# Rounded gate and sigmoid kept as 16-bit halves of a shifted fp32 word, and three-bank evictions, in the quantised feed-forward network at the end of an audio tower

## The chip, the cores and the metric

The kernel runs on one core of one Trainium2 chip. The metric is the device time of one execution in microseconds, from the first to the last instruction with what lies around them. Engines: PE is TensorE (PEld its weight loads), DVE is VectorE, ACT is ScalarE, POOL is GpSimd, SP is the queue that issues the DMAs of this part.

## The reference, cut to what matters

The tower turns audio into 8 x 376 tokens of 256 features, then runs attention, a mixture of experts, a recurrence, and last a feed-forward network in which every step is rounded to 16 bits with one scale for the whole tensor. Only this last network matters here:

```python
def act_qdq(x):
    scale = jnp.maximum(jnp.max(jnp.abs(x)) / 32767, 1e-12)
    return jnp.clip(jnp.round(x / scale), -32768, 32767) * scale
def fixed_qdq_u16(x):
    return jnp.clip(jnp.round(x * 65536), 0.0, 65535.0) / 65536
x = act_qdq(x)
up = act_qdq(x @ dequant(w_up).T)          # 256 -> 768
gate = act_qdq(x @ dequant(w_gate).T)      # 256 -> 768
sig = fixed_qdq_u16(sigmoid(gate))
gate = act_qdq(gate * sig)
o = act_qdq(gate * up)
out = h + o @ dequant(w_down).T            # 768 -> 256
```

Each `act_qdq` needs the largest absolute value of the whole tensor before the first element of it can be rounded. So the network has five points at which everything waits for a peak: x, gate, up, gate*sig and the product with up.

## The kernel before, in words

The last network is the function `quantised_ffn`. A tensor lies as 128 partitions by 6 chunks (QCHUNKS) by 3008 tokens, 8 samples (BATCH) of 376 tokens (TOK). `gate` stays in SBUF whole as fp32. `up` has room for three samples (UPS); the first five samples of it go out to DRAM and come back. Every product on TensorE is three matmuls (high by high, high by low, low by high part). Each engine has its own program; semaphores tie them. A unit is half a sample: 3 chunks, 1128 elements in each partition; there are 16 units.

**Peaks.** `measure` (DVE, L2018 to L2034) reduces the collected peaks, has TensorE turn and spread the top (`share`, L1889 and L1891), and writes a scale and its inverse (L2029, L2030).

**Gate stage.** DVE rounds x by adding MAGIC (1.5 * 2^23; `rounded`, L2038), ACT takes MAGIC off into the high part (`raise_q`, L1939), DVE makes the low part (`lower`, L2043). PE makes the gate in 48 chunks of six matmuls (`chunk`, L1901) into six PSUM banks. ACT evicts each chunk alone (`keep`, L1952), and after the fourth chunk of each sample it makes the high part of the next sample. DVE takes the peak of each sample (`gate_peak`, L2047).

**Sigmoid stage.** PE makes the 48 chunks of `up`. Per unit: ACT adds MAGIC to the scaled gate (`scale_gate`, L1956); DVE takes MAGIC off and scales it back (`ready_gate`, L2061); ACT makes the sigmoid (L1963); POOL multiplies it by 65536 and adds MAGIC (`scale_sig`, L2152); DVE clips it and takes MAGIC off (`ready_sig`, L2067); POOL multiplies gate and sigmoid (`weigh`, L2157); ACT evicts three chunks of `up` (L1952); DVE takes the peak of up (`up_peak`, L2047) and of the gate times sigmoid (`act_peak`, L2072). The sigmoids lie in a ring of four.

**Multiply stage.** Per sample: ACT rounds up (`round_up`, L1970) and gate (`scale_act`, L1974) to packed int16 in `ints`, two buffers each; DVE multiplies them into fp32 (`multiply`, L2079) and takes the peak (`out_peak`, L2083).

**Product stage.** Per sample: DVE rounds (`round_product`, L2089), ACT makes the high part (`high_product`, L1981), DVE the low part (`low_product`, L2094), PE multiplies with the down weights in three token tiles of 18 matmuls each (`product`, L1915), DVE adds the result to the rows loaded late (`result`, L2104), SP stores.

SP stores and reloads `up` in sample order and waits for the same counts of evictions and roundings as ACT makes them.

Of the kernel before, what the change touches and what calls it, by code (L numbers as in the profile page):

```python
# [1784 lines left out]
SIG_STEPS = 65536.0  # L1785
TINY = 1e-12
# [22 lines left out]
def quantised_ffn(nc, psum, norm, up, peaks_x, a, consts, ident, up_gate, down, late_rows, out):  # L1809
# [5 lines left out]
    with ctx:  # L1815
# [9 lines left out]
            .rearrange("p (w u c n) -> p w u c n", w=2, u=2, n=TOK)  # L1825
        gate = sb("q_gate", [P, QCHUNKS, TOKENS])
        peaks = sb("q_peaks", [P, 4, UNITS])
# [4 lines left out]
        steps = sb("q_steps", [P, 12])  # L1832
        (S_X, I_X, S_UP, I_UP, S_GATE, I_GATE, S_ACT, I_ACT, S_BOTH, S_OUT, I_OUT, PEAK) = (
            steps[:, i:i + 1] for i in range(12))
# [7 lines left out]
         gate_scaled, gate_ready, sig_made, sig_scaled, sig_ready, prod_made, act_scaled, up_rounded, out_made,  # L1842
# [3 lines left out]
            "gate_scaled gate_ready sig_made sig_scaled sig_ready prod_made act_scaled up_rounded out_made "  # L1846
# [7 lines left out]
        with nc.Block() as block:  # L1854
            @block.sync
            def _(sp):
                def store(n):
                    u = n % 2
                    sp.wait_ge(result_made, TILES * (n + 1))
                    many, few = token_rows(out, n)  # L1860
                    sp.dma_start(many, late[:, u, 0:2, :]).then_inc(stored[u], 16)
                    sp.dma_start(few, late[0:TILE_ROWS[2], u, 2, :]).then_inc(stored[u], 16)

                for n in range(BATCH - UPS):
                    sp.wait_ge(kept, CHUNKS_ALL + QCHUNKS * (n + 1))
# [70 lines left out]
            def _(act):  # L1936
# [5 lines left out]
                def keep(t):  # L1942
                    n, j = t // QCHUNKS % BATCH, t % QCHUNKS
                    act.wait_ge(made, t + 1)
                    if t < CHUNKS_ALL:
                        dst = gate[:, j, tokens_of(n)]
                    else:
                        dst = up[:, slot(n), j, :]
                        if j == 0 and n >= UPS:
# [8 lines left out]
                def sigmoid(m):  # L1958
                    c, t = half(m)
                    act.wait_ge(gate_ready, m + 1)  # L1960
                    if m >= RING:
                        act.wait_ge(prod_made, m - RING + 1)
                    act.activation(sig[:, m % RING, :, :], gate[:, c, t], ACT.Sigmoid).then_inc(sig_made, 1)  # L1963

                def round_up(k):
                    if k >= UPS:
                        act.wait_ge(up_in[late_slot(k)], 16 * (k // UPS))
                    if k >= 2:
                        act.wait_ge(out_made, k - 1)
                    act.activation(ints[:, 0, k % 2, :, :], up[:, late_slot(k), :, :], ACT.Copy,  # L1970
                                   scale=I_UP).then_inc(up_rounded, 1)
# [5 lines left out]
                def high_product(n):  # L1977
                    act.wait_ge(p_made, n + 1)
                    if n >= 2:
                        act.wait_ge(down_made, TILES * (n - 1))  # L1980
                    act.activation(prod_high[:, n % 2, :, :], shared[:, n % 2, :, :], ACT.Identity,  # L1981
# [23 lines left out]
                for n in range(BATCH):  # L2005
                    high_product(n)

            @block.vector
            def _(dve):
# [40 lines left out]
                def gate_peak(n):  # L2050
                    dve.wait_ge(kept, QCHUNKS * (n + 1))
                    peak_of(GATE_, n, gate[:, :, tokens_of(n)])

                def up_peak(m):
                    dve.wait_ge(kept, CHUNKS_ALL + UNIT * (m + 1))
                    peak_of(UP_, m, up[:, slot(m // 2), half(m)[0], :])

                def ready_gate(m):
                    c, t = half(m)
                    dve.wait_ge(gate_scaled, m + 1)  # L2060
                    dve.tensor_scalar(gate[:, c, t], gate[:, c, t], MAGIC, S_GATE, ALU.subtract,  # L2061
                                      ALU.mult).then_inc(gate_ready, 1)

                def ready_sig(m):
                    s = sig[:, m % RING, :, :]
                    dve.wait_ge(sig_scaled, m + 1)
                    dve.tensor_scalar(s, s, MAGIC + SIG_STEPS - 1, MAGIC, ALU.min, ALU.subtract).then_inc(sig_ready, 1)  # L2067

# [6 lines left out]
                def multiply(k):  # L2075
                    g = gate[:, :, tokens_of(order[k])]
# [9 lines left out]
                def round_product(n):  # L2086
                    if n >= 2:
                        dve.wait_ge(p_low, n - 1)
                    dve.tensor_scalar(shared[:, n % 2, :, :], gate[:, :, tokens_of(n)], I_OUT, MAGIC,  # L2089
                                      ALU.mult, ALU.add).then_inc(p_made, 1)  # L2090

                def low_product(n):
                    dve.wait_ge(p_high, n + 1)
                    dve.scalar_tensor_tensor(prod_low[:, n % 2, :, :], shared[:, n % 2, :, :], MAGIC,  # L2094
                                             prod_high[:, n % 2, :, :].bitcast(F32), ALU.subtract,
# [34 lines left out]
                act_peak(UNITS - 1)  # L2130
                measure(STEP_ACT, peaks[:, ACT_, :], S_ACT, I_ACT, (ranged, UNITS))
                link(dve.tensor_scalar(S_BOTH, S_ACT, S_UP, 1.0 / SIG_STEPS, ALU.mult, ALU.mult))
# [6 lines left out]
                low_product(0)  # L2139
                for n in range(BATCH):  # L2140
                    if n + 2 < BATCH:
                        round_product(n + 2)
                    if n + 1 < BATCH:
                        low_product(n + 1)
                    result(n)

            @block.gpsimd
            def _(pool):
                def scale_sig(m):
                    s = sig[:, m % RING, :, :]  # L2150
                    pool.wait_ge(sig_made, m + 1)
                    pool.tensor_scalar(s, s, SIG_STEPS, MAGIC, ALU.mult, ALU.add).then_inc(sig_scaled, 1)  # L2152

                def weigh(m):
                    c, t = half(m)
                    pool.wait_ge(sig_ready, m + 1)
                    pool.tensor_tensor(gate[:, c, t], gate[:, c, t], sig[:, m % RING, :, :], ALU.mult).then_inc(prod_made, 1)  # L2157

                for m in range(UNITS + 1):
                    if m < UNITS:  # L2160
                        scale_sig(m)
                    if m:
                        weigh(m - 1)
# [142 lines left out]
```

## Time and profile before

| what | value |
|---|---|
| median of 3 runs | 1931.11 us (1928.57 to 1936.67) |
| profiled execution, time | 1944.91 us |
| profiled execution, span | 1943.1 us |
| busy share of the span | PE 82%, PEld 76%, DVE 63%, ACT 52%, POOL 58% |
| mean granted TensorE clock | 0.902 of full speed |

The span runs from the first to the last instruction; the execution's own time is 1.8 us more. The busy shares are means over stages with different limits, so what a change in the last network can bring is read from its own stretch, about 1684 to 1943 us. A granted clock of 1.00 is 2.4 GHz, 0.50 is 1.2 GHz.

### The profile page before, as it was taken

What the parts mean: (1) busy time and instruction counts of PE and PEld (TensorE: products, weight loads), DVE (VectorE), ACT (ScalarE), POOL (GpSimd) and SP (SyncE); (2) the same over time, 40 slices, a digit from 0 to 9 for tenths busy, and PEclk for the clock granted to TensorE, in tenths of its full rate; (3) what the DMA queues carried; (4) which work ended last, traced back from release to release, by engine and by line L of the source; (5) the groups of instructions that cost most, each with busy time, mean ns of one, the idle gap of its engine ahead of it and who ended that gap; (6) DMA issues with size and microseconds to landing.
All of it is one profiled execution on the core that took longest, in us unless ns stands there. A gap on an engine that the chain in (4) does not pass through costs nothing. (4 is left out here: it accounts for less than half of the span.)

```text
span 1943.1 us, 32428 instructions
## 1 busy us (share of the span) xinstructions
PE 1594.4 (82%) x11205; PEld 1479.0 (76%) x11205; DVE 1228.0 (63%) x2392; ACT 1018.9 (52%) x2231; POOL 1120.1 (58%) x859
## 2 busy tenths in 40 slices
PE   7749999999999999997519999999999826698219
PEld 4338898989898989896419999999999825687119
DVE  6756575757575757474624666666655468558886
ACT  3536564647474746473515555554555424459452
POOL 0487676767585858580546767667677646107500
PEclk9859999999999999997559999999999957899659
DMA  5153000000000000000336555555555421003123
GB/s 189 64 188 102 1 8 0 8 0 8 0 8 0 8 8 0 8 2 28 106 113 192 147 143 135 148 136 138 143 151 149 109 77 32 25 1 120 48 87 112
DMA packets 74600, 142.85 MB, mean 74 GB/s; under 512 B 7400, under 2 KB 50728, under 8 KB 73992
## 3 DMA queue, kind: packets, MB, share of 16 engines
q1 hardware_dynamic: 63992, 127.80, 21.0%
q0 software_dynamic: 10512, 13.83, 4.3%
q8 instruction: 53, 0.87, 0.2%
q14 instruction: 43, 0.35, 0.1%
HBM read 108.15 MB, written 46.83 MB: 80 GB/s over the span
## 5 line engine op out<-in xcount | busy, mean ns | idle before, releaser
L1463 POOL TENSOR_TENSOR expert_w_low<-expert_raw,expert_w_high 128x768 fp32r<-128x768 f32 x152 | 289.8, 1959 | 158.4 <-ACT expert_w_high L1322 157.3
L646 ACT ACTIVATE probs<-psum,neg_max 120x376 f32<-120x376 f32 (+2 forms) x384 | 176.3, 479 | 138.6 <-DVE neg_max L763 138.6
L716 POOL TENSOR_TENSOR qk_low<-rotated,qk_high 128x376 fp32r<-128x376 f32 x128 | 138.5, 1082 | 178.7 <-ACT qk_high L639 174.5
L533 PE MATMUL psum<-diag,probs 128*128 128x128 f32 (+2 forms) x1536 | 204.0, 284 | 26.9 <-DVE pt_low L779 22.6
L533 PEld LDWEIGHTS psum<-diag,probs 128*128 128x128 f32 (+2 forms) x1536 | 185.9, 194 | 36.0 <-issue 25.1
L779 DVE TENSOR_TENSOR pt_low<-psum,pt_high 128x752 fp32r<-128x752 f32 x128 | 120.4, 941 | 144.1 <-ACT pt_high L655 143.1
L1439 DVE TENSOR_TENSOR expert_act_low<-expert_act,expert_act_high 128x384 fp32r<-128x384 f32 x152 | 148.3, 976 | 79.6 <-ACT expert_act_high L1360 79.6
L1360 ACT ACTIVATE expert_act_high<-expert_act 128x384 fp32r<-128x384 f32 x152 | 79.8, 525 | 171.4 <-DVE expert_act L1434 171.4
L1281 PE MATMUL psum<-slots_high,expert_w_high 128*128 128x384 f32 x608 | 158.3, 341 | 9.0 <-DVE expert_act L1434 7.8
L1281 PE MATMUL psum<-slots_low,expert_w_high 128*128 128x384 f32 x608 | 155.6, 337 | 0.0
L1281 PE MATMUL psum<-slots_high,expert_w_low 128*128 128x384 f32 x608 | 155.5, 336 | 0.0
L655 ACT ACTIVATE pt_high<-psum 128x752 fp32r<-128x752 f32 x128 | 102.6, 802 | 98.3 <-PE psum L533 96.7
L727 POOL TENSOR_TENSOR rotated<-raw,rope_cos 128x376 f32<-128x376 f32 x128 | 127.5, 996 | 39.3 <-ACT raw L633 25.4
L731 POOL TENSOR_TENSOR rotated<-rotated,swapped 128x376 f32<-128x376 f32 x128 | 138.5, 1082 | 10.0
L1322 ACT ACTIVATE expert_w_high<-expert_raw 128x768 fp32r<-128x768 f32 x152 | 126.6, 833 | 30.3 <-DMA expert_raw<-in_experts 30.3
L1292 PE MATMUL psum<-expert_w_high,expert_act_high 128*128 128x256 f32 x456 | 134.3, 294 | 5.2 <-ACT slot_out L1342 3.8
L1434 DVE TENSOR_TENSOR expert_act<-psum,silu 128x384 f32<-128x384 f32 x152 | 84.6, 557 | 78.6 <-ACT silu L1356 78.2
L729 POOL TENSOR_TENSOR swapped<-swapped,rope_sin 128x376 f32<-128x376 f32 x128 | 132.7, 1037 | 0.0
L1292 PE MATMUL psum<-expert_w_high,expert_act_low 128*128 128x256 f32 x456 | 128.5, 282 | 0.0
L1292 PE MATMUL psum<-expert_w_low,expert_act_high 128*128 128x256 f32 x456 | 128.4, 282 | 0.0
L763 DVE TENSOR_REDUCE neg_max<-psum 120x2 f32<-120x752 f32 (+2 forms) x192 | 119.1, 676 | 4.6 <-PE psum L518 4.6
L550 PE MATMUL psum<-pt_high,v_high 128*128 128x376 f32 (+2 forms) x384 | 114.7, 299 | 1.7 <-DVE pt_low L779 1.7
(304 smaller groups left out, 4633.3 us busy)
## 6 DMA issues: line engine op xcount, KB each, us to landing
expert_raw<-in_experts SPq DMA_DIRECT2D x152, 384.0 KB, 3.1
x_slots<-in_c_slots SPq DMA_DIRECT2D x4, 3168.0 KB, 28.2
slot_rows<-x_slots SPq DMA_DIRECT2D x19, 396.0 KB, 4.4
up_spill<-held SPq DMA_DIRECT2D x5, 1128.0 KB, 5.0
held<-up_spill SPq DMA_DIRECT2D x5, 1128.0 KB, 5.6
patch<-in_patches SPq DMA_DIRECT2D x4, 752.0 KB, 6.7
hid_spill<-hid SPq DMA_DIRECT2D x1, 3008.0 KB, 8.5
resid<-hid_spill SPq DMA_DIRECT2D x8, 376.0 KB, 3.5
```

The source lines that it names most:

```text
L533: last = pe.matmul(psum[0:nj, BANK_PT + bank, at:at + ni], probs[0:ni, h % 2, src:src + nj], diag[0:ni, h % 2, it, 0:ni], start=True, stop ...
L646: last = act.activation(probs[0:ni, h % 2, at:at + P * it + ni], score_bank(h % 2, it), ACT.Exp, bias=neg_max[0:ni, h % 2, it:it + 1], acc ...
L716: pool.tensor_tensor(qk[1][:, c % 2, k, :], rotated[:, k, :], qk[0][:, c % 2, k, :].bitcast(F32), ALU.subtract).then_inc(qk_ready, 1)
L727: pool.tensor_tensor(rotated[:, k, :], raw[:, k, :], cos[:], ALU.mult).then_inc(rope_made, 1)
L729: pool.tensor_tensor(swapped[:, k, :], swapped[:, k, :], sin[:], ALU.mult).then_inc(rope_made, 1)
L731: pool.tensor_tensor(rotated[:, k, :], rotated[:, k, :], swapped[:, k, :], ALU.add).then_inc(rot_made, 1)
L779: dve.tensor_tensor(pt[1][:, h % 2, :, :], psum[:, BANK_PT:BANK_PT + 2, 0:TOK], pt[0][:, h % 2, :, :].bitcast(F32), ALU.subtract).then_inc ...
L1281: last = pe.matmul(psum[:, 2 * k + g % 2, 0:TILE_SLOTS], w[hw][:, f, at:at + P], xt[hx][:, i % 2, c, :], start=(n == c == 0), stop=(n == 2 ...
L1292: last = pe.matmul(psum[:, BANK_DOWN + s, 0:DIM], act_hl[ha][:, g % 2, P * s:P * (s + 1)], w[hw][:, f, 4 * P:4 * P + DIM], start=(n == f = ...
L1322: act.activation(w[0][:, g % RING, :], raw[:, g % RAW, :], ACT.Copy).then_inc(w_high, 1)
L1439: dve.tensor_tensor(act_hl[1][:, g % 2, :], act_f[:, g % 2, :], act_hl[0][:, g % 2, :].bitcast(F32), ALU.subtract).then_inc(low_made, 1)
L1463: pool.tensor_tensor(w[1][:, g % RING, :], raw[:, g % RAW, :], w[0][:, g % RING, :].bitcast(F32), ALU.subtract).then_inc(w_low, 1)
```

## The change

All of it lies in `quantised_ffn`.

- The gate is scaled and MAGIC added as before, but MAGIC is not taken off again. The low 16 bits of the word are the rounded integer: `gate_low` reads them as int16 at a step of two halves. The sigmoid (ACT) reads them with the scale S_GATE.
- The sigmoid is rounded by adding SIG_MAGIC = MAGIC / 65536 = 192 and clipped, in one DVE instruction; the low 16 bits of that word are the integer, read as uint16 (`sig_low`).
- The product of the two halves is now DVE's. POOL has no instruction in this function any more.
- ACT evicts three PSUM banks with one instruction, in both stages; PE signals and waits once in three chunks. The high part of the next sample comes before the first eviction of a sample.
- `scale_act` writes int16 into the low halves of `gate` in place; `ints` holds four roundings of up. The first two roundings of up wait for the scale of up alone.
- The product of the first sample is prepared in two pieces (128 tokens, then 248), and PE waits before each token tile for what it needs.
- The peak of gate*sig is now one of integers, so its `measure` has two more small steps (S_PROD).

```diff
+SIG_MAGIC = MAGIC / SIG_STEPS
+        sig_low = shared[:]...bitcast(mybir.dt.uint16).rearrange("p (r c n w) -> p r c n w", r=RING, c=UNIT, w=2)[:, :, :, :, 0]
+        gate_low = gate[:]...bitcast(mybir.dt.int16).rearrange("p (c n w) -> p c n w", c=QCHUNKS, w=2)[:, :, :, 0]
+        pieces = [(0, 0, P), (0, P, TOK)] + [(n, 0, TOK) for n in range(1, BATCH)]
...
 # PE, chunk(t)
-                    if t >= BANKS:
-                        pe.wait_ge(kept, t - BANKS + 1)
+                    if j % UNIT == 0 and t >= BANKS:
+                        pe.wait_ge(kept, t // UNIT - 1)
...
-                    last.then_inc(made, 1)
+                    if j % UNIT == UNIT - 1:
+                        last.then_inc(made, 1)
 # PE, product(n)
-                    pe.wait_ge(p_low, n + 1)
...
                     for t in range(TILES):
+                        pe.wait_ge(p_low, n + 2 if n or t else 1)
 # ACT
-                    act.activation(dst, psum[:, j % BANKS, 0:TOK], ACT.Copy, scale=S_X).then_inc(kept, 1)
+                    act.activation(dst, psum[:, c, 0:TOK], ACT.Copy, scale=S_X).then_inc(kept, 1)
...
-                    act.activation(sig[:, m % RING, :, :], gate[:, c, t], ACT.Sigmoid).then_inc(sig_made, 1)
+                    act.activation(sig[:, m % RING, :, :], gate_low[:, c, t], ACT.Sigmoid, scale=S_GATE).then_inc(sig_made, 1)
...
-                    act.activation(ints[:, 1, k % 2, :, :], gate[:, :, tokens_of(order[k])], ACT.Copy,
-                                   scale=I_ACT).then_inc(act_scaled, 1)
+                    act.activation(gate_low[:, :, t], gate[:, :, t], ACT.Copy, scale=I_ACT).then_inc(act_scaled, 1)
...
-                for t in range(CHUNKS_ALL):
-                    keep(t)
-                    if t % QCHUNKS == 3 and t // QCHUNKS + 1 < BATCH:
-                        raise_q(t // QCHUNKS + 1)
+                for m in range(UNITS):
+                    if m % 2 == 0 and m // 2 + 1 < BATCH:
+                        raise_q(m // 2 + 1)
+                    keep(m)
                 act.wait_ge(steps_made, STEP_GATE + 1)
                 scale_gate(0)
-                scale_gate(1)
                 for m in range(UNITS):
-                    if m + 2 < UNITS:
-                        scale_gate(m + 2)
+                    if m + 1 < UNITS:
+                        scale_gate(m + 1)
                     sigmoid(m)
-                    for j in range(UNIT):
-                        keep(CHUNKS_ALL + UNIT * m + j)
+                    keep(UNITS + m)
+                act.wait_ge(steps_made, STEP_UP + 1)
+                round_up(0)
+                round_up(1)
                 act.wait_ge(steps_made, STEP_ACT + 1)
-                round_up(0)
                 for k in range(BATCH):
                     scale_act(k)
-                    if k + 1 < BATCH:
-                        round_up(k + 1)
+                    if k + 2 < BATCH:
+                        round_up(k + 2)
 # DVE
-                def ready_gate(m):
...
-                    dve.tensor_scalar(s, s, MAGIC + SIG_STEPS - 1, MAGIC, ALU.min, ALU.subtract).then_inc(sig_ready, 1)
+                    dve.tensor_scalar(s, s, SIG_MAGIC, SIG_MAGIC + 1 - 1 / SIG_STEPS, ALU.add, ALU.min).then_inc(sig_ready, 1)
+                def weigh(m):
...
+                    dve.tensor_tensor(gate[:, c, t], gate_low[:, c, t], sig_low[:, m % RING, :, :], ALU.mult).then_inc(prod_made, 1)
...
-                    dve.tensor_tensor(g, ints[:, 1, k % 2, :, :], ints[:, 0, k % 2, :, :], ALU.mult).then_inc(out_made, 1)
+                    dve.tensor_tensor(gate[:, :, t], gate_low[:, :, t], ints[:, k % RING, :, :], ALU.mult).then_inc(out_made, 1)
...
-                ready_gate(0)
-                ready_gate(1)
-                for m in range(UNITS + 1):
-                    if m + 2 < UNITS:
-                        ready_gate(m + 2)
+                for m in range(UNITS):
+                    ready_sig(m)
                     if m:
-                        ready_sig(m - 1)
-                        up_peak(m - 1)
-                    if m >= 3:
-                        act_peak(m - 3)
+                        act_peak(m - 1)
+                    weigh(m)
+                    up_peak(m)
                 measure(STEP_UP, peaks[:, UP_, :], S_UP, I_UP, (peaked, BATCH + UNITS))
-                act_peak(UNITS - 2)
                 act_peak(UNITS - 1)
-            @block.gpsimd
-                    pool.tensor_scalar(s, s, SIG_STEPS, MAGIC, ALU.mult, ALU.add).then_inc(sig_scaled, 1)
-                    pool.tensor_tensor(gate[:, c, t], gate[:, c, t], sig[:, m % RING, :, :], ALU.mult).then_inc(prod_made, 1)
```

## Rows read from the trace of the kernel before

**Rows 1.** Sigmoid and product stage: PE, PEld, DVE, ACT, POOL busy; clock; DMA, GB/s.

```profile
1745.30:1827.30 82.00, 51.99 (x276) 48.15 (x274) 75.34 (x64) 60.62 (x81) 64.20 (x32) 0.88 0.20 71
1886.40:1939.40 53.00, 52.94 (x432) 52.72 (x432) 35.42 (x36) 13.10 (x6) 0.00 (x0) 0.97 0.32 95
```

**Rows 2.** Chain that ended last, gate stage: start us, duration us, what.

```profile
1684.12 6.32 PE psum L1901 x24
...
1692.88 4.44 PE psum L1901 x24
...
1697.34 0.57 ACT q_gate L1952
1697.92 0.82 ACT q_tokens_high L1939
...
1698.76 0.95 DVE q_tokens_low L2043
...
1699.76 4.43 PE psum L1901 x24
...
1734.02 6.52 PE psum L1901 x36
```

**Rows 3.** ACT: a one-bank eviction, and a two-bank one just before this network.

```profile
L1952 ACT ACTIVATE q_gate<-psum,q_steps 128x376 f32<-128x376 f32 x48 | 27.5, 574 | 25.5 <-PE psum L1901 25.5
L1644 ACT ACTIVATE held<-psum 128x752 f32<-128x752 f32 x8 | 6.4, 797 | 8.3 <-PE psum L1578 8.3
```

**Rows 4.** Timeline of ACT, start of the sigmoid stage: start, duration, then the instruction.

```profile
1745.37 3.77 ACT L1956 ACTIVATE q_gate<-q_gate,consts,q_steps 128x1128 f32<-128x1128 f32 x3 [4.23 <-DVE q_steps L2030]
1749.17 1.28 ACT L1963 ACT_TABLE_LOAD   x1
1750.46 1.14 ACT L1963 ACTIVATE q_shared<-q_gate 128x1128 f32<-128x1128 f32 x1
```

**Rows 5.** Timeline of DVE in the sigmoid stage: its start, middle and end.

```profile
1755.16 0.73 DVE L2067 TENSOR_SCALAR q_shared<-q_shared 128x1128 f32<-128x1128 f32 x1
1755.81 1.32 DVE L2047 TENSOR_REDUCE q_peaks<-held 128x1 f32<-128x1128 f32 x1
...
1768.63 1.11 DVE L2061 TENSOR_SCALAR q_gate<-q_gate,q_steps 128x1128 f32<-128x1128 f32 x1
1769.67 1.29 DVE L2067 TENSOR_SCALAR q_shared<-q_shared 128x1128 f32<-128x1128 f32 x1
1770.88 1.31 DVE L2047 TENSOR_REDUCE q_peaks<-held 128x1 f32<-128x1128 f32 x1
...
1773.35 1.14 DVE L2061 TENSOR_SCALAR q_gate<-q_gate,q_steps 128x1128 f32<-128x1128 f32 x1
...
1827.29 0.15 DVE L2021 TENSOR_REDUCE q_own<-q_peaks 128x1 f32<-128x16 f32 x1
```

**Rows 6.** Timeline of ACT (one row) and DVE around the start of the multiply stage.

```profile
1829.24 2.56 DVE L2072 TENSOR_REDUCE q_peaks<-q_gate 128x1 f32<-128x1128 f32 x2
...
1833.82 2.17 ACT L1970 ACTIVATE q_shared<-held,q_steps 128x2256 int16<-128x2256 f32 x1 [19.06 <-DVE q_steps L2030]
...
1838.15 2.51 DVE L2079 TENSOR_TENSOR q_gate<-q_shared 128x2256 f32<-128x2256 int16 x1 [4.11 <-ACT q_shared L1974]
...
1843.11 2.50 DVE L2079 TENSOR_TENSOR q_gate<-q_shared 128x2256 f32<-128x2256 int16 x1
```

**Rows 7.** Chain that ended last, from the last scale on.

```profile
1880.25 1.41 DVE q_shared L2089
...
1883.88 2.52 DVE q_tokens_low L2094
...
1886.45 52.95 PE psum L1915 x432
```

**Rows 8.** DVE, 384 elements of two SBUF operands, beside POOL's work and without it.

```profile
L1439 DVE TENSOR_TENSOR expert_act_low<-expert_act,expert_act_high 128x384 fp32r<-128x384 f32 x152 | 148.3, 976 | 79.6 <-ACT expert_act_high L1360 79.6
L1425 DVE TENSOR_TENSOR q_raw<-q_raw,q_scale 128x384 f32<-128x384 f32 x12 | 6.7, 558 | 0.4
```

More of the change, by code:

```diff
@@ L1824, in quantised_ffn @@
         ints = shared[:].rearrange("p u c n -> p (u c n)").bitcast(mybir.dt.int16) \
-            .rearrange("p (w u c n) -> p w u c n", w=2, u=2, n=TOK)
+            .rearrange("p (u c n) -> p u c n", u=RING, n=TOK)
+        sig_low = shared[:].rearrange("p u c n -> p (u c n)").bitcast(mybir.dt.uint16) \
+            .rearrange("p (r c n w) -> p r c n w", r=RING, c=UNIT, w=2)[:, :, :, :, 0]
         gate = sb("q_gate", [P, QCHUNKS, TOKENS])
+        gate_low = gate[:].rearrange("p c n -> p (c n)").bitcast(mybir.dt.int16) \
+            .rearrange("p (c n w) -> p c n w", c=QCHUNKS, w=2)[:, :, :, 0]
         peaks = sb("q_peaks", [P, 4, UNITS])
@@ L1831, in quantised_ffn @@
         late = sb("q_late", [P, 2, TILES, DIM])
-        steps = sb("q_steps", [P, 12])
-        (S_X, I_X, S_UP, I_UP, S_GATE, I_GATE, S_ACT, I_ACT, S_BOTH, S_OUT, I_OUT, PEAK) = (
-            steps[:, i:i + 1] for i in range(12))
+        steps = sb("q_steps", [P, 13])
+        (S_X, I_X, S_UP, I_UP, S_GATE, I_GATE, S_ACT, I_ACT, S_BOTH, S_OUT, I_OUT, PEAK, S_PROD) = (
+            steps[:, i:i + 1] for i in range(13))
+        pieces = [(0, 0, P), (0, P, TOK)] + [(n, 0, TOK) for n in range(1, BATCH)]
         magic, minus_magic = consts[:, PLUS_MAGIC:PLUS_MAGIC + 1], consts[:, MINUS_MAGIC:MINUS_MAGIC + 1]
@@ L1940, in raise_q, with keep @@
                                    bias=minus_magic).then_inc(high_made, 1)
[L1942 to L1946, printed above, removed]
-                    else:
-                        dst = up[:, slot(n), j, :]
-                        if j == 0 and n >= UPS:
+                def keep(m):
+                    n, (c, t) = m // 2 % BATCH, half(m % UNITS)
+                    act.wait_ge(made, m + 1)
+                    if m < UNITS:
+                        dst = gate[:, c, t]
+                    else:
+                        dst = up[:, slot(n), c, :]
+                        if m % 2 == 0 and n >= UPS:
                             act.wait_ge(up_out[slot(n)], 16 * (n // UPS))
                             act.wait_ge(peaked, BATCH + 2 * (n - UPS + 1))
-                    act.activation(dst, psum[:, j % BANKS, 0:TOK], ACT.Copy, scale=S_X).then_inc(kept, 1)
+                    act.activation(dst, psum[:, c, 0:TOK], ACT.Copy, scale=S_X).then_inc(kept, 1)
                 def scale_gate(m):
@@ L1959, in sigmoid @@
                     c, t = half(m)
-                    act.wait_ge(gate_ready, m + 1)
+                    act.wait_ge(gate_scaled, m + 1)
                     if m >= RING:
                         act.wait_ge(prod_made, m - RING + 1)
-                    act.activation(sig[:, m % RING, :, :], gate[:, c, t], ACT.Sigmoid).then_inc(sig_made, 1)
+                    act.activation(sig[:, m % RING, :, :], gate_low[:, c, t], ACT.Sigmoid, scale=S_GATE).then_inc(sig_made, 1)
                 def round_up(k):
@@ L1967, in round_up, with high_product @@
                         act.wait_ge(up_in[late_slot(k)], 16 * (k // UPS))
-                    if k >= 2:
-                        act.wait_ge(out_made, k - 1)
-                    act.activation(ints[:, 0, k % 2, :, :], up[:, late_slot(k), :, :], ACT.Copy,
+                    if k >= RING:
+                        act.wait_ge(out_made, k - RING + 1)
+                    act.activation(ints[:, k % RING, :, :], up[:, late_slot(k), :, :], ACT.Copy,
                                    scale=I_UP).then_inc(up_rounded, 1)
                 def scale_act(k):
-                    act.activation(ints[:, 1, k % 2, :, :], gate[:, :, tokens_of(order[k])], ACT.Copy,
-                                   scale=I_ACT).then_inc(act_scaled, 1)
-                def high_product(n):
-                    act.wait_ge(p_made, n + 1)
+                    t = tokens_of(order[k])
+                    act.activation(gate_low[:, :, t], gate[:, :, t], ACT.Copy, scale=I_ACT).then_inc(act_scaled, 1)
+                def high_product(i):
+                    n, lo, hi = pieces[i]
+                    act.wait_ge(p_made, i + 1)
                     if n >= 2:
                         act.wait_ge(down_made, TILES * (n - 1))
-                    act.activation(prod_high[:, n % 2, :, :], shared[:, n % 2, :, :], ACT.Identity,
+                    act.activation(prod_high[:, n % 2, :, lo:hi], shared[:, n % 2, :, lo:hi], ACT.Identity,
                                    bias=minus_magic).then_inc(p_high, 1)
@@ L2075, in multiply @@
                 def multiply(k):
-                    g = gate[:, :, tokens_of(order[k])]
+                    t = tokens_of(order[k])
                     dve.wait_ge(act_scaled, k + 1)
                     dve.wait_ge(up_rounded, k + 1)
-                    dve.tensor_tensor(g, ints[:, 1, k % 2, :, :], ints[:, 0, k % 2, :, :], ALU.mult).then_inc(out_made, 1)
+                    dve.tensor_tensor(gate[:, :, t], gate_low[:, :, t], ints[:, k % RING, :, :], ALU.mult).then_inc(out_made, 1)
                 def out_peak(k):
@@ L2117, in _ @@
                 measure(STEP_GATE, peaks[:, GATE_, 0:BATCH], S_GATE, I_GATE, (peaked, BATCH))
-                ready_gate(0)
-                ready_gate(1)
-                for m in range(UNITS + 1):
-                    if m + 2 < UNITS:
-                        ready_gate(m + 2)
+                link(dve.tensor_scalar(S_PROD, S_GATE, 1.0 / SIG_STEPS, None, ALU.mult))
+                for m in range(UNITS):
+                    ready_sig(m)
                     if m:
-                        ready_sig(m - 1)
-                        up_peak(m - 1)
-                    if m >= 3:
-                        act_peak(m - 3)
+                        act_peak(m - 1)
+                    weigh(m)
+                    up_peak(m)
                 measure(STEP_UP, peaks[:, UP_, :], S_UP, I_UP, (peaked, BATCH + UNITS))
-                act_peak(UNITS - 2)
                 act_peak(UNITS - 1)
-                measure(STEP_ACT, peaks[:, ACT_, :], S_ACT, I_ACT, (ranged, UNITS))
-                link(dve.tensor_scalar(S_BOTH, S_ACT, S_UP, 1.0 / SIG_STEPS, ALU.mult, ALU.mult))
+                measure(STEP_ACT, peaks[:, ACT_, :], S_ACT, I_ACT, (ranged, UNITS), S_PROD)
+                link(dve.tensor_tensor(S_BOTH, S_ACT, S_UP, ALU.mult))
                 for k in range(BATCH):
@@ L2139, in _ @@
                 low_product(0)
+                round_product(2)
+                low_product(1)
                 for n in range(BATCH):
                     if n + 2 < BATCH:
-                        round_product(n + 2)
+                        round_product(n + 3)
                     if n + 1 < BATCH:
-                        low_product(n + 1)
+                        low_product(n + 2)
                     result(n)
-            @block.gpsimd
[L2148 to L2151, printed above, removed]
-                    pool.tensor_scalar(s, s, SIG_STEPS, MAGIC, ALU.mult, ALU.add).then_inc(sig_scaled, 1)
-                def weigh(m):
-                    c, t = half(m)
-                    pool.wait_ge(sig_ready, m + 1)
-                    pool.tensor_tensor(gate[:, c, t], gate[:, c, t], sig[:, m % RING, :, :], ALU.mult).then_inc(prod_made, 1)
[L2159 to L2163, printed above, removed]
 def audio_tower(nc, a, out):
```

38 lines of the change are left out of this document (19 added, 19 removed).

## The prediction

> **What bounds the kernel now.** I read the stretches first, then the chain of waits that ended last, then the timelines of DVE and ACT where the chain sits on them. Nothing before 1684 us changes, so only the last network counts. The chain shows four stages in it, each bounded by something else.
>
> Gate stage: 48 chunks of six matmuls. The reader is to see that a sample takes 6.88 us (1692.88 to 1699.76), though 36 matmuls without a break take 6.52 us [rows 2]: the last ones of a sample are waited out because ACT made the next high part only after the fourth eviction, and DVE the low part behind it.
>
> Sigmoid stage: DVE is busy 75.3 of 82.0 us and PE only 52.0 [rows 1]. From 1768.63 to 1773.35 stands one period of 4.72 us with four DVE instructions and no gap [rows 5]. POOL is busy 64.2 us beside it [rows 1], and the same `ready_sig` that occupies DVE for 1.21 us in the middle (1769.67 to 1770.88) took 0.65 us at the start (1755.16 to 1755.81), when POOL had nothing to do [rows 5].
>
> Multiply stage: DVE again, multiply and peak, one sample in 4.96 us (1838.15 to 1843.11) [rows 6].
>
> Product stage: PE without a break, 52.95 us for 432 matmuls, behind a lead of 6.20 us (1880.25 to 1886.45) in which it has nothing [rows 7].
>
> **The change part by part.**
>
> *Gate stage.* One matmul takes (6.52 - 4.43) / 12 = 0.174 us, so a sample 6.27 us if nothing stops PE [rows 2]. Is it stopped? After the change DVE does per sample rounding, a peak and a low part, some 4.1 us; ACT a high part (0.82 [rows 2]) and two evictions. The next low part is ready 1.2 (eviction) + 2.5 (peak) + 0.95 = 4.7 us into a sample, before the 6.27 are over. Two halves of three banks are enough, since a half is evicted in about 1.2 us and needed again after 3.1. So PE runs through: the first sample at the low clock takes 6.32 + 12 x 0.174 = 8.4 us, seven more 43.9: 52.3 against 56.4 now (1684.12 to 1734.02 + 6.52). Gain 4.1. The last eviction is longer. One bank takes 0.57 us, two 0.80 [rows 3]; a third adds at least the 0.22 between these and at most a whole 0.57, so 1.0 to 1.4, and I take 1.2, because ACT takes 1.26 for 1128 elements of SBUF (3.77 / 3 [rows 4]). That is 0.6 later. **Net -3.5 us.**
>
> *Sigmoid stage.* Now it runs from 1745.37 to 1827.29 [rows 4, 5], 81.9 us. Its start: two `scale_gate` (2.5), the table load (1.28), a sigmoid (1.14) [rows 4]: DVE begins 5.0 us in. Per unit DVE then has
> - `ready_sig` without POOL: 0.65, against 1.21 now [rows 5];
> - `weigh`, new on DVE. No row has an operand of 16-bit halves at a step of two. The nearest is the multiplication of packed int16 into fp32, 2.51 us for 2256 elements [rows 6], so half of it, 1.25. Its bounds: not below 0.65 (the fastest DVE pass over 1128 elements in the trace [rows 5]), and above twice the row, 2.5, if halves at a step were read at half speed. I take 1.25, as the element count is the same and the bytes spanned are those of fp32;
> - two peaks, 1.23 each [rows 5]. `ready_gate` (1.04) is gone.
>
> Sum 4.36 us against 4.72. The first unit has no `act_peak` and waits some 0.3 for the second sigmoid: 3.4; fifteen more 65.4. With the start 73.8. **-8.1 us.** What covers the rest: ACT has 1.26 + 1.04 + 1.2 = 3.5 us in a unit, PE 18 x 0.174 = 3.1, so neither is next; the next is ACT, 0.9 behind. The sigmoid waits for the `weigh` four units back, which DVE has then done. The stores of `up` go by counts that are reached as before, and a slot is wanted again only three samples (26 us) later. The extra link for S_PROD lies in DVE's wait for the first sigmoid.
>
> *Start of the multiply stage.* From the last peak of up (1827.29 [rows 5]) to the first multiplication (1838.15 [rows 6]) are 10.86 us: 1.95 for the scale, then two peaks of 1.28 each on DVE, a second scale, and then two ACT roundings (1833.82 to 1838.15, 4.33). After: ACT rounds `up` twice as soon as the scale of up stands, and the scale of the act needs one peak, 2.0 and two more small steps, in all about 3.7 us, under the 4.2 of the two roundings. So 1.95 + 3 roundings (6.4) = 8.35. **-2.5 us.** The two steps of S_PROD thus cost nothing; without that cover they would be 0.4. The reloads of `up` start earlier by as much, and none of the five was waited for before.
>
> *Multiply stage.* DVE again has both instructions per sample, 4.96 us. `multiply` reads one operand at a step; bounds as above, taken at its row. ACT, writing halves at a step, has two roundings of 2.07, 4.14 us, and 0.8 of slack. **0.**
>
> *Product stage.* For 128 tokens (768 elements a partition) the lead is rounding 0.6 (L2089's 1.41 cut to a third), high part 0.85, low part 0.95 (the 752-element ones took 0.82 and 0.95 [rows 2]), with waits 2.6 us against 6.20. DVE's next steps, two roundings and the low part of 248 tokens, end about 5.5 us after the scale. PE's first 18 matmuls, at the low clock, took 3.7 us of the 52.95, so they end at 6.3: no new wait. If the second piece were late, each us would count. After that the order is that of before. **-3.6 us.**
>
> *Evictions and signals.* 96 evictions become 32 and PE's waits a third. All of it is on ACT and PE, which bound no stage but the first, where it is counted.
>
> Sum: 3.5 + 8.1 + 2.5 + 3.6 = 17.7 us. The profiled execution has a span of 1943.1 and took 1944.91 us; it would take 1927.2. The median of the runs is 13.8 us under it; I take the same 17.7 from the median, 1931.11: **1913.4 us**.
>
> **The rules.** `ready_sig` at 0.65 rests on POOL being the cause of the 1.21. A second place shows the same for two operands: 384 elements took 976 ns beside POOL and 558 without it [rows 8]. The Trainium skill (SBUF — State Buffer, Who interferes with whom) says that GpSimd and a two-port VectorE instruction take one port pair in turns, each for a whole instruction; by that the 1.21 goes with POOL. On 16-bit operands at a step the Trainium skill (Advanced Engine Details and Errata, SBUF Cachelines) says full speed as long as successive accesses share a 16-byte line; a step of 4 bytes does, so by it the sum stays 17.7. No row here tests it.
>
> **The rivals.**
> - *Halves at a step are read slowly on DVE.* At twice the time `weigh` adds 1.25 x 16 = 20 us and `multiply` 2.5 x 8 = 20, both on the engine that bounds its stage: 1913.4 + 40 = 1953.4, slower than before. It decides from a factor of 1.44 on. For it: no row has such an operand. Against: packed 16-bit, fp32 and peaks all go at one element in about 1.1 ns. Chance 0.05.
> - *ACT writes or reads halves slowly.* `scale_act` at 4.1 makes ACT 6.2 per sample against 4.96: 6 x 1.25 + 2.1 = 9.6; the sigmoids at 2.1 make ACT 4.5 a unit against 4.36, 2 us and 1 at the start. 1926. Chance 0.05.
> - *POOL was not the cause.* `ready_sig` stays at 1.21: 16 x 0.56 = 9 us: 1922.4. Against it are the two pairs of rows named. Chance 0.05.
> - *PE takes over in the sigmoid stage.* It now waits for three banks at once. At the lower of its two clocks 18 matmuls take at least three quarters of the 6.32 of the first 24 [rows 2], 4.7, and at most twice 3.13, 6.3, both over 4.36; I take 5.5. The granted clock of the stage is 0.88, with PE busy 63% [rows 1]; with a shorter period PE is busier, 71%. If it stayed low for all: (5.5 - 4.36) x 15 = 17 us, so 1931, no change. Chance 0.04.
> - That the change does not do what it says would be seen as POOL instructions in the stage; the diff leaves none.
>
> **How the numbers follow.** The forecast has 0.81. About 0.5% (9.7 us) is what a measurement of this kernel tells from no change; faster means under 1921.5. All of the forecast and a part of the POOL rival lie there: 0.83. Same: the rest of that rival, the ACT and PE ones, 0.12. Slower: the first rival, 0.05. The range: down by 2 us for eviction and periods and 5 for the spread of the runs, whose lowest lies 2.5 under the median, 1906; up to the ACT rival, 1926. Left out are the DVE and PE rivals and a tail below.
>
> **What would show it.** No POOL in the stretch; DVE's `ready_sig` at about 0.73 and `weigh` at about 1.3; a period of 4.36 in the sigmoid stage; PE in the gate stage without gaps; three-bank evictions at 1.2; the first multiplication 8.4 us after the last peak of up; PE starting 2.6 us after the last scale. A `weigh` or `multiply` at double length, or gaps in DVE's row of the sigmoid stage, would make the prediction wrong.

## The result, and the profile after

The changed kernel takes 1913.97 us (median of 4 runs, 1912.91 to 1914.82), the kernel before 1931.56 us in the same comparison: a ratio of 0.9911, 95% interval 0.9899 to 0.9923, so 17.6 us or 0.9% less. The forecast was 1913.4. One execution of kernel 11 below took 2693.7 us at a granted clock of 0.551 and is left out of its median.

The two profiled spans lie 30.1 us apart (1943.1 and 1913.0), more than the change is worth. Counted from the first gate matmul to the end of the last product, the network took 255.3 us before (1684.12 to 1939.40 [rows 2, 7]) and takes 238.3 now (1671.08 to 1909.34). The other 13 us lie ahead of it, in code that is the same in both: the profiled execution before was itself 13 us above the median of the kernel before, the one after 1 us above its own. The changed kernel run again in another set (kernel 12 below) bears this out: its network took 238.2 us as here, but began at 1677.98 in place of 1671.08, with the same code ahead of it. So the length of the network repeats, and the time at which it begins does not. Where those microseconds arise was not found.

The chain that ended last, kernel after, from the gate stage on (start us, duration us, what):

```profile
1671.08 51.96 PE psum L1907 x288
...
1728.51 2.55 ACT q_gate L1963 x2
...
1731.08 1.28 ACT L1970
...
1732.37 1.24 ACT q_shared L1970
...
1754.65 0.65 DVE q_shared L2069
1755.30 1.24 DVE q_peaks L2079
1756.54 1.24 DVE q_gate L2074
1757.78 1.24 DVE q_peaks L2055
1759.02 0.66 DVE q_shared L2069
...
1802.74 0.18 DVE q_own L2029
...
1804.71 4.24 ACT q_shared L1977 x2
1808.95 2.69 ACT q_gate L1982
...
1811.72 2.52 DVE q_gate L2086
...
1853.83 0.63 DVE q_shared L2097
...
1856.46 52.88 PE psum L1922 x432
```

PE now makes all 288 gate matmuls in one piece, where it stopped once in each sample before [rows 2]. The sigmoid stage is a strict round of four DVE instructions, 4.37 us a unit, and none of them is stretched as `ready_sig` was in [rows 5]. Between the last peak of up (1802.74) and the first multiplication (1811.72) stand the scale of up (1.97 us) and three ACT roundings, two of up in 4.24 us and then `scale_act` in 2.69. The product stage begins 2.63 us after the last scale [rows 7].

Groups of the same kernel, last network, ACT and DVE. Behind the bar stand the busy time in us and the mean of one instruction in ns, then the idle time before them:

```profile
L1982 ACT ACTIVATE q_gate<-q_gate,q_steps 128x2256 int16<-128x2256 f32 x8 | 22.1, 2776 | 0.0
L1959 ACT ACTIVATE q_gate<-psum,q_steps 128x1128 f32<-128x1128 f32 x16 | 19.3, 1204 | 27.6 <-PE psum L1907 27.6
L2074 DVE TENSOR_TENSOR q_gate<-q_gate,q_shared 128x1128 f32<-128x1128 int16 x16 | 21.1, 1321 | 0.0
L2086 DVE TENSOR_TENSOR q_gate<-q_gate,q_shared 128x2256 f32<-128x2256 int16 x8 | 20.0, 2500 | 3.1 <-ACT q_gate L1982 3.1
L2069 DVE TENSOR_SCALAR q_shared<-q_shared 128x1128 f32<-128x1128 f32 x16 | 11.8, 735 | 5.1 <-ACT q_shared L1970 5.0
```

The reader is to see that DVE reads halves at a step as fast as packed ones (2500 ns for 2256 elements, as before), that a three-bank eviction takes 1.20 us against 0.57 for one bank [rows 3], and that ACT's write of halves takes 2.78 us where the packed one of the kernel before took 2.16.

Stage by stage, in us:

| stage | before | after | forecast of the difference | measured |
|---|---|---|---|---|
| gate, first matmul to the scale of the gate | 61.25 | 57.43 | -3.5 | -3.8 |
| sigmoid | 81.9 | 74.2 | -8.1 | -7.7 |
| last peak of up to first multiplication | 10.86 | 8.98 | -2.5 | -1.9 |
| multiply, to the last scale | 42.10 | 42.11 | 0 | 0.0 |
| lead of the product | 6.20 | 2.63 | -3.6 | -3.6 |
| 432 matmuls | 52.95 | 52.88 | 0 | -0.1 |

Sum: -17.0 measured in the stages, -17.7 forecast, -17.6 between the medians.

### The profile page after: what moved, and what is told of

It is laid out like the page before. It is cut to its first block and busy times, and to the rows that moved or that the text cites. A ratio compares the mean times of both kernels' runs of the same rounds, so it can differ in the third digit from the quotient of the medians.

```text
span 1913.0 us, 32335 instructions
## 1 busy us (share of the span) xinstructions
PE 1589.7 (83%) x11205; PEld 1476.6 (77%) x11205; DVE 1221.8 (64%) x2397; ACT 1011.1 (53%) x2168; POOL 1055.0 (55%) x827
## 5 line engine op out<-in xcount | busy, mean ns | idle before, releaser
L533 PEld LDWEIGHTS psum<-diag,probs 128*128 128x128 f32 (+2 forms) x1536 | 185.5, 194 | 36.2 <-issue 25.5
```

The source lines that it names most:

```text
L533: last = pe.matmul(psum[0:nj, BANK_PT + bank, at:at + ni], probs[0:ni, h % 2, src:src + nj], diag[0:ni, h % 2, it, 0:ni], start=True, stop ...
```

## The experiments

The chips of the three sets differ: the kernel before took 1931.6, 1943.4 and 1939.9 us on them. So runs are set against the kernel before by their ratio, and stages against stages. The ratios are those of the record, which can lie 0.0005 off the quotient of two medians.

**1. POOL given two instructions per unit, on a scratch tile** (the result is unaffected; ACT waits for the last of them before it rounds up).

```diff
+ pool.wait_ge(sig_made, m + 1)
+ pool.tensor_scalar(idle, idle, 1.0, 0.0, ALU.mult, ALU.add)
+ pool.wait_ge(sig_ready, m + 1)
+ pool.tensor_tensor(idle, idle, idle, ALU.mult)
```

> The changed kernel, with POOL given back its two instructions per unit in the sigmoid stage, but on a scratch tile that nobody reads (a tensor_scalar and a tensor_tensor of 1128 fp32 elements each). Theory (POOL's work takes a port that DVE's two-port and two-operand instructions need): ready_sig rises from 0.65 us to 1.2 or more, weigh, which starts while POOL is in its 2.6 us multiplication, waits up to 1.4 us, and the sigmoid stage grows from 74.2 us by 9 us at least and about 20 us at most; the kernel takes 1923 to 1934 us. Rival (the shorter ready_sig of the changed kernel has another cause, its other operations say): nothing changes, ready_sig stays at 0.65 and the kernel within 0.2% of 1914 us.

Measured: 1932.03 us against 1931.62, ratio 1.0004 (0.9995 to 1.0014), so as slow as the kernel before. The sigmoid stage takes 90.9 us (1726.90 to 1817.78), 16.7 more. That this equals the gain of the whole change is a coincidence: the change took only 7.7 us out of this stage, and the other stages kept what they had gained. Timelines of DVE (four rows), then POOL (two rows), this kernel:

```profile
1770.36 1.32 DVE L2082 TENSOR_REDUCE q_peaks<-q_gate 128x1 f32<-128x1128 f32 x1
1771.60 2.54 DVE L2077 TENSOR_TENSOR q_gate<-q_gate,q_shared 128x1128 f32<-128x1128 int16 x1
1774.06 1.31 DVE L2058 TENSOR_REDUCE q_peaks<-held 128x1 f32<-128x1128 f32 x1
1775.30 0.73 DVE L2072 TENSOR_SCALAR q_shared<-q_shared 128x1128 f32<-128x1128 f32 x1
```

```profile
1770.88 2.07 POOL L2165 TENSOR_TENSOR q_late<-q_late 128x1128 f32<-128x1128 f32 x1 [1.33 <-DVE q_shared L2072]
1773.04 2.09 POOL L2162 TENSOR_SCALAR q_late<-q_late 128x1128 f32<-128x1128 f32 x1
```

POOL's multiplication began at 1770.88 and ended at 1772.95; `weigh` was issued at 1771.60 and ended at 1774.14, 1.19 us after that, which is about its own length. All fifteen `weigh` that lay beside POOL's multiplication ended 1.18 to 1.20 us behind it, most of them with a length of 2.25 us. The peak of one operand beside it (1.32) lost nothing. So the theory holds, though the two share no data. `ready_sig` mostly escaped: it stays at 0.73 here, because it begins at 1775.30, when POOL's second instruction has just ended (1773.04 + 2.09). Only in the first two units did it lie beside POOL's work. DVE (two rows), then POOL (two rows), same kernel:

```profile
1732.10 1.72 DVE L2072 TENSOR_SCALAR q_shared<-q_shared 128x1128 f32<-128x1128 f32 x1 [5.05 <-ACT q_shared L1972]
...
1736.34 1.37 DVE L2072 TENSOR_SCALAR q_shared<-q_shared 128x1128 f32<-128x1128 f32 x1
```

```profile
1732.09 1.13 POOL L2162 TENSOR_SCALAR q_late<-q_late 128x1128 f32<-128x1128 f32 x1 [83.13 <-ACT q_shared L1972]
1733.97 3.14 POOL L2165 TENSOR_TENSOR q_late<-q_late 128x1128 f32<-128x1128 f32 x1 [0.75 <-DVE q_shared L2072]
```

Both times `ready_sig` ended 0.60 us after POOL's instruction. In the kernel before, each `ready_sig` that lay beside POOL did the same: the one of 1769.67 [rows 5] ended at 1770.96, 0.60 us after a POOL instruction that ran from 1768.92 to 1770.36. The length of `ready_sig` thus follows POOL's instruction and not its own operations, which differ between the two kernels. The sum closes: `weigh` was busy for 36.2 us in the stage in place of 21.1 and `ready_sig` for 13.3 in place of 11.8, together 16.6 of the 16.7 us. The Trainium skill (SBUF — State Buffer, Who interferes with whom) has GpSimd and a two-port VectorE instruction take the shared ports in turns, each for a whole instruction; the rows of `ready_sig` agree, 0.60 us behind POOL's end.

**2. `ready_sig` alone on POOL**, and **3. the same without its minimum** (the clip at 65535 is left out). In both, DVE's order in a unit is now `weigh`, `up_peak`, `act_peak`.

```diff
- dve.tensor_scalar(s, s, SIG_MAGIC, SIG_MAGIC + 1 - 1 / SIG_STEPS, ALU.add, ALU.min)
+ pool.tensor_scalar(s, s, SIG_MAGIC, SIG_MAGIC + 1 - 1 / SIG_STEPS, ALU.add, ALU.min)   # 2
+ pool.tensor_scalar(s, s, 1.0, SIG_MAGIC, ALU.mult, ALU.add)                            # 3
```

> The changed kernel, with ready_sig alone on POOL, so that DVE has three instructions per unit (3.72 us) and POOL one. Theory (DVE's instruction time sets the sigmoid stage, and one POOL instruction of 1.1 to 1.5 us can lie beside the peaks): the period falls from 4.37 to 3.75 us, the stage by some 9 us, and the kernel to about 1905 us. Rival (port): weigh waits for POOL's instruction each time, the period stays at 4.4 or more and the kernel within 0.2% of 1914 us. Second rival (ACT, at 3.5 to 3.7 us a unit, takes over): a period of 3.7 to 3.9.

> As the run with ready_sig on POOL, but its instruction multiplies by 1 and adds (the form that scale_sig had) and leaves the clip at 65535 out. Theory A (POOL's minimum made that instruction 4 us long and POOL the bound): it takes 1.1 to 2.1 us, POOL is no longer the bound, the period falls to between 3.75 us (no wait at the port) and 4.8 us (weigh waits for POOL each time); I expect about 4.3, with weigh at 1.3 to 2, and a kernel within 0.4% of 1914 us. Theory B (POOL waits for DVE, whatever its operation): the instruction stays above 4 us and the kernel at 1927 us.

Measured: 2 takes 1927.21 us, ratio 0.998 (0.9971 to 0.999), and its network 251.4 us, 13 more than the changed kernel's. None of its three theories foresaw why. The chain of kernel 2 at the start of the sigmoid stage, where POOL is alone, and a stretch of POOL's timeline:

```profile
1734.39 4.04 POOL q_shared L2151
```

```profile
1761.49 23.91 POOL L2151 TENSOR_SCALAR q_shared<-q_shared 128x1128 f32<-128x1128 f32 x5
```

POOL's add-and-minimum takes 4.04 us for 1128 elements while DVE is idle, and five in a row 23.9, 4.78 each: POOL is the bound. Kernel 3 settles it (theory A, POOL's minimum makes it long): its multiply and add takes 1.14 us. (The multiplication by 1 came in as the minimum went, so what is shown slow is add with minimum as a pair.) The kernel has ratio 0.9885 (0.9868 to 0.9901), the sigmoid stage 66.6 us (1741.85 to 1808.45), the network 230.9. Its timelines of POOL and of DVE:

```profile
1760.77 1.14 POOL L2151 TENSOR_SCALAR q_shared<-q_shared 128x1128 f32<-128x1128 f32 x1 [2.29 <-ACT q_shared L1970]
...
1777.95 2.37 POOL L2151 TENSOR_SCALAR q_shared<-q_shared 128x1128 f32<-128x1128 f32 x1 [1.34 <-ACT q_shared L1970]
```

```profile
1770.57 1.32 DVE L2069 TENSOR_TENSOR q_gate<-q_gate,q_shared 128x1128 f32<-128x1128 int16 x1
...
1774.28 1.32 DVE L2069 TENSOR_TENSOR q_gate<-q_gate,q_shared 128x1128 f32<-128x1128 int16 x1
```

The period is 3.71 us, three DVE instructions, better than the 4.3 expected. Of its sixteen `weigh` only one was held up (1.99 us); the others lay clear of POOL's instruction, or it was POOL's that grew (1.14 to 2.37), and POOL has time. With experiment 1 this says that DVE sets the stage and what POOL may do beside it: one short instruction, not two that fill the period.

**4 and 5. Is the step what makes ACT's write slow?** In 4 `scale_act` writes packed int16 to a tile of its own; in 5 `round_up` writes halves at a step, too, though into another tile than it reads. In both, roundings of up have two buffers in place of four, and ACT makes the second `scale_act` ahead of the third `round_up`.

```diff
- act.activation(gate_low[:, :, t], gate[:, :, t], ACT.Copy, scale=I_ACT)
+ act.activation(ints[:, 1, k % 2, :, :], gate[:, :, t], ACT.Copy, scale=I_ACT)          # 4
+ ints = shared[:]...bitcast(int16).rearrange("p (u c n w) -> p u c n w", u=2, c=QCHUNKS, w=2)[:, :, :, :, 0]  # 5
```

> The changed kernel, with scale_act writing packed int16 into a tile of its own, as before the change. Theory (halves written at a step of four bytes are slower on ACT): scale_act takes 2.16 us again in place of 2.77, the first multiplication comes 8.4 us after the last peak of up in place of 9.0, the multiply stage stays at 42.1 us, and the kernel gains 0.6 us, too little for the median. Rival (scale_act is slow for another reason, say its place beside DVE's work on gate): it stays at 2.77.

> The changed kernel, with round_up, too, writing halves at a step of four bytes, into a tile other than the one it reads. Theory (the step is the cause): round_up takes 2.77 us in place of 2.15; with both at 2.77, ACT has 5.3 us per sample against DVE's 4.96 and the multiply stage grows by 1 to 3 us. Rival (writing into the tile that is read is the cause): round_up stays at 2.15 and the stage at 42.1. In both, multiply with both operands at a step stays at 2.5 us if DVE does not mind the step.

Measured: 4 took 1914.40 us, 5 took 1915.48 (one run each). ACT groups of 4, then of 5:

```profile
L1982 ACT ACTIVATE q_shared<-q_gate,q_steps 128x2256 int16<-128x2256 f32 x8 | 17.2, 2160 | 0.0
```

```profile
L1977 ACT ACTIVATE q_shared<-held,q_steps 128x2256 int16<-128x2256 f32 x8 | 22.1, 2775 | 18.3 <-DVE q_steps L2039 18.3
```

Packed 2.16, at a step 2.78 in either place: the step is the cause, not the writing in place. DVE's `multiply` took 2500 ns in both, with no operand at a step in 4 and with both in 5. In 4 the first multiplication comes 8.4 us after the last peak of up, in 5 10.1, since all three roundings ahead of it are long there. The expected growth of the multiply stage itself did not come in 5: ACT's 2 x 2.64 = 5.3 us a sample are over DVE's 4.96, but ACT had the second sample ready some 2.4 us before DVE wanted it, and the six samples behind it use up about 0.32 each, so the stage took 42.1 us.

**6. The early high part alone**, on the kernel before.

```diff
-                    if t % QCHUNKS == 3 and t // QCHUNKS + 1 < BATCH:
+                    if t % QCHUNKS == 0 and t // QCHUNKS + 1 < BATCH:   # and ahead of keep(t)
```

> The kernel before, with one thing of the change: the high part of the next sample is made before the first eviction of a sample, not after the fourth; evictions stay one bank each. Theory (the order of ACT's program made PE wait at each sample): PE runs through the gate stage, 288 matmuls in 52 us in place of 56.4, and the kernel gains 4.1 us, 0.2%. Rival (the longer, fewer evictions and signals are what lets PE run): the stage stays at 56.4 us and the kernel at the time of before.

Measured: ratio 0.9978 (0.997 to 0.9987), 3.7 us of 1943.4 between the medians, and in its chain PE in one piece for the gate:

```profile
1680.77 51.94 PE psum L1901 x288
1732.73 0.58 ACT q_gate L1952
```

The order of ACT's program gives all of the gate stage's gain (56.4 us of PE to 51.9); with one-bank evictions the tail behind it is 0.6 us shorter than with three. The three-bank evictions give nothing there.

**7 and 8. Late roundings of up; whole first sample.** In 7 the first two `round_up` stand behind the scale of the act; in 8 the first sample of the product stage is one piece.

> The changed kernel, with the first two roundings of up behind the scale of the act, as the first one was before. Theory: these two (4.2 us) come onto the path; from the last peak of up to the first multiplication 1.95 + 3.7 + 4.2 + 2.7 = 12.5 us in place of 9.0, so 3.5 us more. Rival (the time goes by the scale of the act, not by ACT's roundings): 9.0 us or at most 1 us more.

> The changed kernel, with the first sample of the product stage prepared whole, as before. Theory (the lead is on the path): from the last scale to the first matmul 6.2 us in place of 2.6, 432 matmuls in 53 us as before, 3.6 us more in all. Rival (the first matmuls run at the low clock anyway, so part of the earlier start is given back): the lead grows by 3.6 but the 432 matmuls are shorter by 1 us or more.

Measured: in 7 the first multiplication comes 12.7 us after the last peak of up (8.98 with the change). The 3.7 us between them are the time to the scale of the act, which lay under the first two roundings with the change and lies ahead of them in 7. In 8 the chain reads

```profile
1865.27 1.40 DVE q_shared L2097
1866.70 2.18 ACT q_tokens_high L1989
1868.91 2.52 DVE q_tokens_low L2103
1871.47 52.82 PE psum L1922 x432
```

6.20 us of lead and 52.8 of matmuls: all 3.6 us are the split's, and the 432 matmuls (52.88 with it) give nothing back. (One run each, 1929.86 and 1929.80 us on slower chips; the stages are what is compared.)

**9 to 12. Versions meant to beat both.** 9 (best_dve) adds four small things to the changed kernel. 10 adds to these the rounding on POOL by conversion to uint16, which is relied on to round and to saturate (whether it saturates no run here shows by itself); 11 the POOL instruction of experiment 3 instead, without the clip; 12 is the changed kernel again.

```diff
+ act.activation(steps[0:1, 13:14], steps[0:1, 13:14], ACT.Sigmoid)      # 9: before the wait for STEP_GATE
+ sigmoid(m) ahead of scale_gate(m + 1); scale_act packed; last gate_peak in two halves
+ pool.tensor_scalar(sig_low[:, m % RING, :, :], s, SIG_STEPS, 0.0, ALU.mult, ALU.add)   # 10
```

> The changed kernel with four small things: scale_act packed into a tile of its own (-0.6 us); a one-element sigmoid before the wait for the scale of the gate, so that the table load (1.28 us) lies in that wait; sigmoid(0) ahead of scale_gate(1) (-1.25); the peak of the last gate sample in two halves, so that only 1.25 in place of 2.5 us lie behind the last eviction. If each is on the path, 4.4 us in all, 1909.6 us, and a ratio to the changed kernel of 0.998. Rival: DVE's start in the sigmoid stage is then paced by ACT, which has three instructions per unit, and 1 to 2 us of it come back.

> The changed kernel itself, unaltered, on the same chip and in the same rounds as the next two, so that they can be set against it. Its ratio to the kernel before was 0.9911; I expect 0.990 to 0.992 again. It also tests whether the profiled execution's gain beyond the last network (30 us of span against 17 in the stages) belongs to the change: by the theory that it does not, every profile here shows the last network 17 us shorter than before, while the start of it varies with the chip.

> The four small things of the run before and, in addition, the rounding of the sigmoid on POOL in one instruction that multiplies by 65536 and writes uint16 at a step, with rounding and saturation left to the conversion, so that neither the shift nor a minimum is needed. Theory: POOL takes 1.1 to 2.4 us as in the run that only added, DVE's period is 3.71, the sigmoid stage falls from 74.2 to about 64 us and the kernel to 0.984 to 0.986 of the kernel before. Rival: the conversion to 16 bits costs POOL as much as the minimum did (4 us), and the period is 4.8: slower than the changed kernel by about 8 us.

> The same with POOL's fp32 multiply-and-add, leaving the clip at 65535 out: the sigmoid stage at about 64 us, the kernel at 0.984 to 0.986 of the kernel before. If the four small things and POOL's rounding do not add up, it stays above 0.987.

| run | median us | ratio to the kernel before, 95% | sigmoid stage us | network us |
|---|---|---|---|---|
| 9 | 1922.21 | 0.9894 (0.9877 to 0.9911) | 71.8 | 234.4 |
| 12, changed kernel | 1923.76 | 0.9914 (0.9901 to 0.9928) | 74.2 | 238.2 |
| 10 | 1912.82 | 0.9858 (0.9843 to 0.9874) | 64.9 | 227.5 |
| 11 | 1912.19 | 0.9852 (0.9834 to 0.987) | 64.1 | 227.0 |

Run 9 belongs to the second set, the others to the third. Run 10 is 10.9 us faster than the changed kernel in the same set (1912.82 to 1923.76), and 1.4% faster than the kernel before. Its groups of POOL and DVE:

```profile
L2156 POOL TENSOR_SCALAR q_shared<-q_shared 128x1128 uint16<-128x1128 f32 x16 | 27.5, 1721 | 104.9 <-ACT q_shared L1970 104.9
```

```profile
L2071 DVE TENSOR_TENSOR q_gate<-q_gate,q_shared 128x1128 f32<-128x1128 int16 x16 | 22.3, 1396 | 4.1 <-POOL q_shared L2156 4.1
```

The conversion costs POOL 1.5 to 2.5 us, not 4, and DVE's `weigh` is held up little (1396 ns against 1321): one of sixteen was, by 1.2 us. In run 9 the table load lies before the scale, and DVE begins 2.7 us after the scale in place of 5.2. Its network is 3.8 us shorter than the changed kernel's, where 4.4 were expected: 2.4 in the sigmoid stage, 1.2 ahead of it and 0.6 at the start of the multiply stage, less 0.4 by which the 432 matmuls were longer. Its ratio (0.9894) does not stand clear of the changed kernel's 0.9911; that it is faster is read from the stages, not shown by the times.

## Why the prediction was right

*What bounds each stage* held throughout. Experiments 6, 7 and 8 each changed one term alone (the gate stage, the start of the multiply stage, the lead of the product) and moved it by about what the prediction had for it; experiments 1 and 3 moved the sigmoid stage through DVE's instructions; and the multiply stage stayed at 42.1 us in 4 and 5, whatever ACT's roundings took.

*Gate stage*: 51.96 us of PE against 52.3, eviction 1.20 as taken. The gain was put down to the order of ACT's program and not to the number of evictions; experiment 6 shows both.

*Sigmoid stage*: `ready_sig` 0.65 and `weigh` 1.24 us as forecast, period 4.37 (4.36). The start was 5.2 us, not 5.0 (the first sigmoid took 1.24 us, not 1.14); the rest of the missing 0.4 is mostly 0.01 in each period. The change pays in this stage only because the port comes free: with `ready_sig` at its old 1.21 the period would be 4.93 by an estimate (4.37 + 0.56), longer than the 4.72 of before. The rival "POOL was not the cause" fell with experiment 1, and the rival of slowly read halves on DVE with the groups above. PE did not take over: the stage's period stayed DVE's, and the granted clock of the stage was 0.90 against 0.88 before.

*Start of the multiply stage*: here a term was mis-sized. "1.95 + 3 roundings (6.4) = 8.35" took `scale_act` at its packed length; it is 2.78 us long (2.69 on the chain), so 8.98. The ACT rival named the mechanism, at twice the time; it is 1.28 times (2.64 against 2.07 us from one start to the next). On the path it costs once, 0.6 us; in the stage it lies in ACT's slack (4.70 against DVE's 4.96), as the prediction's cover had it. The Trainium skill (Advanced Engine Details and Errata, SBUF Cachelines) has full performance where successive accesses hit the same 16-byte line, which by the prediction's reading covers a step of four bytes. For DVE's reads the rows agree; for ACT's writes of halves they do not, 2.78 against 2.16 us, and the measurement decides.

*Product stage*: lead 2.63 against 2.6, no wait behind the first tile. The parts fit less well than their sum: a third of 1.41 us is 0.47, not the 0.6 that the prediction took and the trace shows (0.63), and the high part took 0.95 us, not 0.85.

The profile of before had a span 13 us too long in parts that do not change. Taking the difference from the stages and subtracting it from the median was what kept this out of the forecast. That 17.7 and 17.6 us lie so close is in part luck: the interval of the ratio stands for 15 to 20 us, and in the stages two terms gained less than forecast (0.4 and 0.6 us) and one more (0.3), for 17.0 in all.

## What to carry to other kernels

Take the period of a stage from the instructions of the engine that bounds it, and ask of each whether it is long by itself or because another engine holds its port; moving an instruction to the bounding engine can pay if it frees that port. What another engine costs is set by how the two fall together: the same two POOL instructions left fourteen of sixteen `ready_sig` alone and held up fifteen of sixteen `weigh`. A serial start (a scale, a table load, a first rounding) is on the path even where the stage behind it hides everything, so work that needs only an earlier scale goes ahead of the wait for the next one, and the first piece is cut small. POOL can carry one short instruction beside such a stage, if its operation is one that it does fast.

## What the runs showed of the hardware that was not expected

- ACT writing 2256 16-bit halves at a step of four bytes took 2.78 us, packed 2.16, in place or not; DVE reading them took the same 2.50 as packed.
- POOL's tensor_scalar over 1128 fp32 elements took 1.14 us for multiply and add, 1.48 with uint16 out at a step, and 4.04 for add and minimum.
- POOL's conversion from fp32 to uint16 could stand in for the shift and the rounding (kernel 10).
- A DVE instruction with two SBUF operands started beside POOL's multiplication took 2.24 to 3.18 us in place of 1.32 (kernel 1), always ending about 1.19 us behind it; a peak of one operand lost nothing.
